# The last tile's store issued as nine transfers instead of one

## The reference

```python
def reference(x, itok_B_0_7, L0_cond_weights):
    ...
        w = weights[subjects]
        out = jnp.einsum('bct,bcd->bdt', x, w)
        return out
    x = x + _L0_cond_ref(x, itok_B_0_7, L0_cond_weights)
    return x
```

## Time and profile before

| | us |
|---|---|
| three runs | 325.48, 327.03, 327.35 |
| median | 327.03 |
| the profiled execution's own time | 326.79 |
| its span, first to last instruction | 324.8 |
| ACT issues the last store, in the span | 309.80 |

### The profile page before, as it was taken

The page is one execution under the profiler, slowest core; times in us unless marked ns, Lnnn a source line. Parts: engine busy times, 40 slices in busy tenths (PEclk is TensorE's granted clock), DMA queues, the critical chain, the costliest instruction groups (busy, mean ns, idle before and its releaser), DMA issues.

```text
span 324.8 us, 4203 instructions
## 1 busy us (share of the span) xinstructions
PE 239.8 (74%) x1032; PEld 111.6 (34%) x1032; DVE 160.2 (49%) x130; ACT 130.0 (40%) x129; POOL 52.7 (16%) x137
## 2 busy tenths in 40 slices
PE   3499999999787787786776867768768677687600
PEld 1145555554243343342332332323323333333200
DVE  0437767767546446355354464453544645535410
ACT  1026646556434334334244243342443433424400
POOL 2132122222111111111111011111110111100000
PEclk9979999999999999999999999999999999999955
DMA  7999999999999999999999999999999999999992
GB/s 267 423 422 423 425 427 427 426 426 428 427 428 428 427 427 428 427 428 425 430 424 430 424 428 427 428 427 427 427 428 426 429 426 427 428 426 428 427 428 123
DMA packets 19478, 134.78 MB, mean 415 GB/s; under 512 B 2066, under 2 KB 3091, under 8 KB 3091
## 3 DMA queue, kind: packets, MB, share of 16 engines
q1 hardware_dynamic: 10256, 67.64, 49.7%
q10 hardware_dynamic: 9218, 67.11, 49.0%
HBM read 67.63 MB, written 67.11 MB: 415 GB/s over the span
## 4 chain that ended last, share of the span: by engine, by line
PE 73%; DVE 11%; ACT 5%; issue 2%; DMA 1%; DVEq 1%; POOL 1%; POOLq 1%; ACTq 0%
PE products L140 72%; DVE out_ring L168 10%; ACT out_ring L189 5%; DMA loaded<-weights 1%; DVE table L153 1%; PE products L123 1%; DVEq L37 1%; POOL selected L112 1%; POOLq L107 0%; POOLq L112 0%; ACTq L187 0%; POOLq L101 0%; DVEq L173 0%; POOLq L111 0%; DVEq L152 0%
## 5 line engine op out<-in xcount | busy, mean ns | idle before, releaser
L140 PE MATMUL products<-x_ring,selected 64*128 64x512 f32 x1024 | 234.2, 601 | 61.9 <-DVE out_ring L168 35.0
L168 DVE COPY out_ring<-products 64x1024 f32<-64x1024 f32 x128 | 156.4, 1222 | 140.2 <-PE products L140 138.2
L189 ACT COPY out_ring<-products 64x1024 f32<-64x1024 f32 x128 | 128.7, 1006 | 177.6 <-PE products L140 176.1
L140 PEld LDWEIGHTS products<-x_ring,selected 64*128 64x128 f32 x1024 | 109.3, 188 | 186.7 <-issue 139.3
L112 POOL COPY selected<-table 64x256 f32 x128 | 51.0, 398 | 234.8 <-PE products L140 177.9
L123 PE MATMUL products<-loaded,spread 128*128 128x512 f32 x8 | 5.7, 876 | 5.4 <-DMA loaded<-weights 5.4
L153 DVE TENSOR_TENSOR table<-products,unit 128x1024 f32<-128x1024 f32 x2 | 3.8, 1942 | 9.2 <-PE products L123 9.2
L123 PEld LDWEIGHTS products<-loaded,spread 128*128 128x128 f32 x8 | 2.2, 295 | 8.0 <-issue 8.0
L189 ACT ACT_TABLE_LOAD x1 | 1.3, 1283 | 1.5 <-PEq L210 1.5
L96 POOL TENSOR_SCALAR_AFFINE_SELECT unit<-ones 64x256 f32<-64x256 f32 x2 | 0.8, 404 | 0.1
L88 POOL TENSOR_SCALAR_AFFINE_SELECT spread<-ones 128x256 f32<-128x256 f32 x1 | 0.4, 419 | 0.1
## 6 DMA issues: line engine op xcount, KB each, us to landing
x_ring<-x SPq DMA_DIRECT2D x64, 1024.0 KB, 35.0
out<-out_ring ACTq DMA_DIRECT2D x64, 1024.0 KB, 35.5
loaded<-weights SPq DMA_DIRECT2D x1, 512.0 KB, 4.3
subject_row<-subjects ACTq DMA_DIRECT2D x1, 0.5 KB
```

Of the source, the lines that this page charges most:

```text
L140: last = nc.tensor.matmul(products[:, b, g, n * BANK:(n + 1) * BANK], selected[part, k, e * mixed:(e + 1) * mixed], x_ring[part, s, e * ti ...
L168: nc.vector.tensor_copy(out_ring[0:HALF, s, b * times:(b + 1) * times], products[b * HALF:(b + 1) * HALF, s % PSUM_BUFS, 0, :]).then_inc(e ...
L189: nc.scalar.copy(out_ring[HALF:channels, s, b * times:(b + 1) * times], products[b * HALF:(b + 1) * HALF, s % PSUM_BUFS, 1, :]).then_inc(o ...
```

## The change

The store of the last tile of the last turn is issued by ACT as nine transfers, of rows 0 to 63, 64 to 99, 100 to 106, 107 to 112, 113 to 117, 118 to 121, 122 to 124, 125 to 126, and row 127. The same bytes go to the same places. ACT's last turn is written out for this and its loop now has six turns in place of seven. The semaphore `stored[7]` counts eight transfers more, 16 for each, and the wait at the end asks for them. Nothing else is changed: the other engines have the same instructions as before.

```diff
+SPLIT_TILES = 1
+ENDS = [0, 64, 100, 107, 113, 118, 122, 125, 127, 128]
+PARTS = list(zip(ENDS, ENDS[1:]))
...
-            def go_round(turn, first=False):
+            def go_round(turn, first=False, last=False):
...
-                    act.dma_start(out_rows[bass.ds(tile * channels, channels), :],
-                                  out_ring[:, s]).then_inc(stored[s], DMA)
+                    for a, b in PARTS if last and s >= TILES_PER_TURN - SPLIT_TILES else [(0, channels)]:
+                        act.dma_start(out_rows[bass.ds(tile * channels + a, b - a), :],
+                                      out_ring[a:b, s]).then_inc(stored[s], DMA)
 
             go_round(0, first=True)
-            with act.Fori(1, turns) as turn:
+            with act.Fori(1, turns - 1) as turn:
                 go_round(turn)
+            go_round(turns - 1, last=True)
             for s in range(TILES_PER_TURN):
-                act.wait_ge(stored[s], turns * DMA)
+                extra = len(PARTS) - 1 if s >= TILES_PER_TURN - SPLIT_TILES else 0
+                act.wait_ge(stored[s], (turns + extra) * DMA)
```

## The result

Over 18 runs of each the changed kernel took 328.85 us and the kernel before 327.0, both medians. The ratio, which goes by the means and leaves out one slow execution of the changed kernel (331.53 us), is 1.0048, with a 95% interval from 1.0024 to 1.0071. That is 1.6 us more (0.8 to 2.3), not 1.2 us less. The range of 325.0 to 328.2 didn't hold it. The sign was wrong.

The account below looks back on a forecast made before the run. The prediction took the kernel as bound by bytes on sixteen full DMA engines, its end by one late engine's queue. Four rows fewer there, 1.22 us, other terms nothing: 327.03 - 1.22 = 325.8 us, range 325.0 to 328.2.

Parts of the forecast that it names:

- What bounds the end: After 319 us: one late DMA engine works through its own queue, some 4.9 us or 16 rows behind the rest.
- The division of rows: Last tile's store: 14 to 8 rows on the first seven engines, 7 on the next five, 4 on the last four.
- Which engine is late: End of the stores: late engine taken as one of the last four, 4 rows instead of 8, 1.22 us less.
- that rival: Last tile's store: late engine gets 9 to 14 rows, 0.3 to 1.84 us more, 327.3 to 328.9 us; chance 0.13.
- Parts read at full speed: Last tile's parts: each engine still takes 0.306 us per row, though a part covers half the memory's rows.
- Slow reading: Rival at the last tile's parts: read at down to half speed, 327.0 to 328.3 us; chance 0.24.
- half the traffic: Reason for full speed at the last tile's parts: loads are over by then, and half the traffic with them.
- Eight issues of 0.34 us, hidden with 3.8 us to spare: ACT's extra issues at the last tile: at most 2.7 us, over by about 312.8, before engines arrive at 316.6; cost nothing.
- The written-out turn: ACT's longer program: one more instruction packet would cost 0.3 us on the late engine, one in sixteen; otherwise nothing.
- got rows: Sign of a wrong forecast, at the end: a single engine that ends after 323.9 us.
- The sign for slow reading: DMA share well below 1 between 316.6 and 318.5 us while all engines have rows.
- the two slow cases: At the last tile's store: parts read slowly, 327.0 to 328.3, chance 0.24; late engine with more rows, 327.3 to 328.9, 0.13.

Follow-up runs that it names:

- e1: Changed kernel with ACT's last turn written out, but the last tile's store as one transfer of 128 rows: 326.59 us, ratio 0.9994 to the kernel before.
- e5: Changed kernel with the last tile's store as two 64-row parts, even rows then odd rows: 326.86 us, ratio 0.9992 to the kernel before.
- e9: Changed kernel with the last tile's store as four 32-row parts, each taking every fourth row: 326.84 us, ratio 0.9999 to the kernel before.
- e4: Changed kernel with the last tile's store in parts of 64, 25, 25 and 14 rows: 330.78 us, ratio 1.0109 to the kernel before.
- e2: Changed kernel with the last tile's store as two halves of 64 neighbouring rows: 328.02 us, ratio 1.0029 to the kernel before.
- e6: Changed kernel with the last tile's store as four parts of 32 neighbouring rows: 328.61 us, ratio 1.0042 to the kernel before.
- e3: Changed kernel with the last tile's store in parts of 60 and 68 rows: 326.89 us, ratio 0.9997 to the kernel before.
- e8: Changed kernel, but the last four tiles each stored as 112 rows and four times 4 rows: 330.91 us, ratio 1.0156 to the kernel before.
- e12: The changed kernel once more, unchanged, with a second trace: 328.89 us, ratio 1.0059 to the kernel before.
- e7: Changed kernel with nine parts of the change's sizes, but taking every second row: 329.58 us, ratio 1.0076 to the kernel before.

## Why the prediction was wrong, point by point

- **What bounds the end.** One engine with a queue of its own sets the end: right. It did so in both traces of the changed kernel. 8 rows on it made no change in e1, e5 and e9, and 15 rows in e4 made 3.6 us more. Rows alone don't give the time, though: e2 and e6 have 8 as well and took 0.9 and 1.4 us more.
- **The division of rows.** 14, 13, 12 ... 4: right as far as seen. Ten rows with five completions is exactly its fifth entry, and the small packets rise by 39 where it gives 40. The rule of the Trainium skill, DMA: Bandwidth & Descriptors, section on why a DMA increments its semaphore by 16, on the largest divisor agrees with this trace, with e3 and with e4. That the engines used are the lowest-numbered ones no record here can show.
- **Which engine is late: the step that failed.** "I choose about six in ten for the last four, a choice that no row makes." It was the fifth. It has 10 rows and not 4: 0.6 us more in the last step instead of 1.2 less, a swing of 1.8 us. The choice rested on a habit that no row shows, and the rows of before can't tell the engines apart. The Trainium skill, DMA: Bandwidth & Descriptors, in its table on latency and other measured facts, has engines 7 and 15 as the usually slower ones. This case doesn't agree, if the engines are numbered as the rule on the division has it: the late one is then engine 4, in every trace that tells. The honest weight was the count, 6 in 16 for the first six. I gave that rival 0.13. Its range (327.3 to 328.9) holds the measured 328.6, but in part by luck: for ten rows its price is 0.6 us, so 327.6, and the other 1.0 is the next point.
- **Parts read at full speed: the second step that failed.** Slow reading was held as the strongest rival, and was right in kind. But the place was another: I had the late engine's own four rows and the first engine's fourteen slowed. What moved the end was the whole stores ahead, still in the late engine's queue while the others were at their parts: 0.8 us in one trace, 1.3 in the other. The reason given for full speed, that "half the traffic" ends with the loads, was misread: with the loads over, the engines still moved 428 GB/s from 310 to 315 us. The Trainium skill, SBUF — State Buffer, section on door 1, has the rule that neighbouring rows reach fewer ports. It agrees with e6 against e9 (1.4 us against none, same sizes and counts) and with e2 against e5. That the late engine's rows are slowed by others at the same port is argued from it, not shown; part of the slowing comes when the others have ended.
- **Eight issues of 0.34 us, hidden with 3.8 us to spare.** Mis-sized: 0.92 us in the median, 8.79 for the nine. The cover was gone, the narrow parts came late, and the bulk ended near 322 in place of 320.8; slow rows have a share in that too. The late issues cost nothing at the end, since the late engine still had a backlog: the last one was over by 319.7, and its ten rows followed each other in 3.1 us from 324.3. With four tiles split they have a part in the 5.1 us of e8.
- **The written-out turn.** Nothing, right within the interval (e1).
- **The sum with the measured terms.** 0.6 for the rows and 0.8 to 1.3 for the slowed stores give 1.4 to 1.9 us; measured 1.6 (0.8 to 2.3) over 18 runs and 1.9 (1.0 to 2.9) in e12.
- **The signs.** The sign that it "got rows", a single engine that ends after 323.9, came. The sign for slow reading, a share well below 1, couldn't: a slow row keeps its engine busy, and the share stood at 1.03 from 315 to 318.5 and at 1.09 with 328 GB/s at 319. GB/s beside the share is what shows it.
- **The range.** Its top was at 328.2, cut just below the tops of the two slow cases. Rows added to the late engine and slow reading could also come together, and they did.

What stays open: why the fifth engine is late at all; why rows of the late engine are slow when no other engine is at work any more, the one row of 1.58 us in e7 included; and what makes the stretch at 20 to 40 us slow in some executions, the same kernel's included.

## What to carry to other kernels

Before moving work off a straggler, find out which one it is: a pair of cheap kernels that put extra rows on the first n and the first n + 1 engines tells it, and here two runs would have turned the sign of the forecast. A store cut into parts of neighbouring rows can slow transfers ahead of it that it doesn't touch, while two or four equal parts that step over the whole memory cost nothing that shows. Where a term is chosen without a row, give the other cases the weight of their count.

## What the runs showed that I had not expected

- A transfer issued right behind another takes ACT about 1 us and up to 1.7 in the changed kernel, against 0.34 for a single one. In e8 the first five took 2.99 us and the third five 7.08.
- Two or four parts with every second or fourth row cost no more than one (0.9992 and 0.9999); the same number of parts of neighbouring rows cost 0.9 and 1.4 us.
- A full busy share of the DMA engines can move 339 instead of 426 GB/s for some microseconds in the body of an execution; that came and went between executions of one kernel and is worth 1.6 us, as much as the change.
